# New due times, lags and look-ahead for the planner that orders an attention and expert-routing kernel

## The chip, the cores and the metric

One core of one Trainium2 chip runs the whole program. The metric is the device time of one execution in microseconds, as the median of several runs; a profile of one further execution shows where the time lies.

## The reference, cut to what matters

The input `x` is 8 batches of 512 tokens of 512 numbers in float32. The layer is cross-attention followed by a routed feed-forward part:

```python
def reference(x, ctx, mask, Wq, bq, Wk, bk, Wv, bv, Wo, bo, Ws, bs, W1, b1, W2, b2):
    xn = layernorm(x)                                 # per token
    q, k, v = xn @ Wq + bq, ctx @ Wk + bk, ctx @ Wv + bv
    # 16 heads of 32; sim = q k^T / sqrt(32), masked by key
    x = x + softmax(sim) @ v @ Wo + bo
    xf = layernorm(x).reshape(4096, 512)
    route_prob = softmax(xf @ Ws + bs).T              # 8 experts x 4096 tokens
    route_vals, routes = top_k(route_prob, 512)       # each expert takes 512 tokens
    h = gelu(einsum('ekd,edf->ekf', xf[routes], W1) + b1)      # 2048 wide
    y = (einsum('ekf,efd->ekd', h, W2) + b2) * route_vals
    return x + scatter_add(y at routes)
```

## The kernel before, in words

**Two stages.** The attention stage handles all 8 batches and also writes the normalised rows and the routing logits; the expert stage then picks each expert's tokens, gathers them and runs the two expert products. Every float32 operand of a product is split into a high and a low part (names ending in hi and lo), and a product is three matmuls: high by high, low by high, high by low. The expert stage isn't touched by the change.

**The unit of the attention stage is a group** of four heads of one batch: 32 groups, g = 4b + r for batch b. For a group there are these steps, each of which may have a part on several engines:
- `proj` k and q (lines 1883 to 1885): 12 matmuls each in four chunks; ScalarE makes the high part (line 1266), VectorE the low part (line 1475); SyncE stores both in HBM (`keep_hi`, `keep_lo`, lines 954 and 961) and loads them again in a stacked layout (`stack_hi`, `stack_lo`, lines 985 and 996; `mask_row`, line 971).
- `max`, 16 tiles (line 1901): scores of queries by keys; VectorE takes the extremum of each row (line 1490) and ScalarE the sum of exponentials (`sum`, line 1289).
- `rows` (line 1918): the 16 columns of extrema are turned into rows; ScalarE (line 1280) and VectorE (line 1498, `rows_lo`) split them, and GpSimd issues two small DMAs (line 1183) that put them under the stacked queries. The first `score` of the group waits for these.
- `score`, 16 tiles (line 1933), whose exponentials ScalarE makes (line 1301), and `att`, four steps of four matmuls each (line 1944; eight records a step in the trace), that add into one bank; `recip`, `rden` (line 1925), `divide` (line 1522) and `osplit` (lines 1310 and 1546) finish the group.

**Per batch** come four tiles each of: `load c`, `csplit` (ScalarE line 1246, VectorE line 1426) for the context; `load x`, `stats` (VectorE lines 1394 to 1398, then GpSimd line 1043), `norm` (line 1403), `turn` (PE line 1843) for the queries' input; `v`; and after the batch's groups `residual` (line 1114), `add_bias` (line 1141), `outa` and `out` (PE lines 1960 to 1962, VectorE lines 1554 and 1562 with statistics behind the latter), `x1_norm`, `route` (PE line 1975), `logits` (line 1986) and `back` (line 1994). The loads of c, x and residual share four slots in turn (line 1103 for c and x): a c tile of batch b can only be loaded when the residual tile of batch b - 2 has been routed and its normalised row stored (SyncE line 1018).

**What sets the order.** Each engine executes its steps in the order of a list, in program order, and waits on semaphores. The list comes from a planner in Python that runs when the kernel is built (`Plan`, `attention_agenda`). Every step has a due time counted in groups, a cost on its engine and a time until others see its result (`COST`), and the steps it comes after. Steps of one kind on one engine form a line in order of due time; in the simulated time of the planner, an engine takes, of all heads of lines that can start within `LOOK` microseconds of the earliest, the one that is due first. So due times decide only where several steps are ready together. PSUM banks are given out by the same plan, and at most three `max` and two `score` tiles are held at a time (`HELD`). The due time of a step is its place in `K_AT`, `Q_AT`, `MAX_AT` (one pair for each place of a group in its batch) or `SPAN` (group offset, first and last of the four tiles), plus the engine's `LAG` for that line. The costs are fixed numbers. The steps before group 0's first scores are written out by hand (`first_steps`), and the change doesn't reach them.

```python
first = min(start for start, _ in able)
start, part = min((p for p in able if p[0] <= first + LOOK), key=lambda p: (p[1].at, p[0]))
```

Of the kernel before, what the change touches and what calls it, by code (L numbers as in the profile page):

```python
# [71 lines left out]
class Plan:  # L72
# [14 lines left out]
    def run(self):  # L87
# [36 lines left out]
        while left:  # L124
            best = None
            for engine in a.order:
# [7 lines left out]
                if able:  # L134
                    first = min(start for start, _ in able)
                    start, part = min((p for p in able if p[0] <= first + LOOK), key=lambda p: (p[1].at, p[0]))
                    if best is None or start < best[0]:
# [128 lines left out]
def first_steps(a):  # L266
# [101 lines left out]
             "piece_in": (0.800, 3.00)},  # L368
}
STATISTICS = (1.020, 1.10)  # L370
LOOK = 0.0482
HELD = {"max": 3, "score": 2}
LAG = {
    ("act", "proj"): 0.05484, ("dve", "proj_lo"): 0.02698, ("pool", "rows_lo"): -0.63573, ("act", "rows"): 0.02773, ("dve", "rows_lo"): -0.36946,
    ("sync", "stack_hi"): -0.05651, ("sync", "stack_lo"): 0.367, ("pool", "recip"): -0.23075, ("dve", "rden"): -0.1455, ("dve", "outa"): -0.82589,
    ("dve", "csplit_lo"): 0.10561, ("dve", "turn_lo"): 0.12437, ("dve", "v"): 0.35108, ("dve", "out"): 0.28505, ("act", "turn"): -0.2497,
    ("dve", "back"): 0.11423, ("act", "osplit"): -0.38468, ("dve", "divide"): 0.38329, ("act", "logits"): -0.64673, ("pool", "add_bias"): -0.82451,
    ("act", "csplit"): -0.35997, ("pe", "rows"): 0.22469, ("dve", "route"): -0.24839, ("dve", "max"): -0.0842, ("dve", "recip"): 0.22088,
    ("act", "score"): 0.05782, ("act", "sum"): 0.03391, ("pe", "score"): -0.3388, ("dve", "osplit_lo"): 0.25044, ("sync", "den_in"): 0.01022,
    ("sync", "den_out"): -0.08642,  # L380
}
K_AT = ((0.29686, 0.40376), (-0.04542, 0.29441), (0.02773, 0.08012), (-0.31589, 0.13175))
Q_AT = ((0.44226, 0.47919), (0.23484, 0.31819), (0.08741, 0.37171), (0.25863, 0.4367))
MAX_AT = ((-0.0746, 0.65113), (-0.03252, 0.72888), (-0.08586, 0.78647), (0.28673, 0.73702))
ROWS_AT, RECIP_AT, RDEN_AT, OSPLIT_AT, ATT_AT = -0.39061, 0.33435, 1.07093, -0.39162, 0.06092
SPAN = {
    "v": (-1, 0.20496, 1.61489), "load_c": (-3, -0.37589, 0.1772), "csplit": (-3, -0.77777, -0.28119), "load_x": (-3, 0.70516, 0.81243),
    "stats": (-3, 0.5984, 0.6084), "norm": (-3, 0.59116, 1.14657), "turn": (-3, 0.37171, 0.50368), "residual": (2, -0.16222, 0.44313),
    "add_bias": (2, 1.63304, 2.37175), "outa": (2, 0.17666, 1.03948), "out": (4, 0.05675, 0.7842), "x1_norm": (4, 0.60213, 1.17617),
    "route": (4, 0.40306, 1.08729), "logits": (4, 0.55598, 1.13947), "back": (4, 0.74368, 1.13342),  # L390
}


def spread(span, k, n):
    return span[0] + (span[1] - span[0]) * (k + 0.5) / n


def attention_agenda():
# [48 lines left out]
    for g in range(NG):  # L447
# [3 lines left out]
        if g >= 2:  # L451
            for w in "kq":
                span = (K_AT if w == "k" else Q_AT)[before]
                turned = [("dve", "turn_lo" if w == "q" else "csplit_lo", b, t) for t in range(TB)]
# [15 lines left out]
        if g >= 1:  # L470
            stacks = [("sync", "stack_" + k, w, g) for k in ("hi", "lo") for w in "kq"] + [("sync", "mask_row", g)]
            for n in range(AHEAD if g == 1 else 0, HG * TB):
                h, t = divmod(n, TB)
                at = g - 1 + spread(MAX_AT[(g - 1) % GB], n, HG * TB)
                p.add("pe", ("max", g, h, t), at, stacks if n == 0 else [], takes=("max", g, h, t))
# [1737 lines left out]
```

## Time and profile before

| | |
|---|---|
| Median of 3 runs | 1664.97 us (1664.57 to 1665.52) |
| Time of the profiled execution | 1665.4 us |
| Its span in the profile | 1663.6 us |
| Granted TensorE clock, mean share | 0.985 |
| TensorE busy | 1596.0 us (96%) |
| VectorE busy | 1120.7 us (67%) |
| ScalarE busy | 979.1 us (59%) |
| GpSimd busy | 299.8 us (18%) |
| First score of group 0, divide of group 31 | 51.63 us, 877.25 us |

Times are counted from the span's start. A busy share of TensorE counts overlapping records, so a stretch of 96% isn't one in which nothing can be gained, and small gaps are better read from single rows. The profiled execution took 1.8 us more than its span, and lies 0.4 us above the median.

### The profile page before, as it was taken

The numbers are of one execution on the slowest core, as the hardware profiler recorded it, in microseconds if no ns is written. First come the engines' busy times: TensorE is split into PE (matmuls) and PEld (weight loads), VectorE is DVE, ScalarE is ACT, GpSimd is POOL, SyncE is SP. The second block draws the span as 40 slices with busy tenths as digits, with TensorE's granted clock in tenths as the row PEclk, the third lists the DMA queues.
The fourth block names the chain that finished last, engine by engine and source line by source line (L and its number), as shares of the span: only waits on it lengthen the run. The fifth ranks groups of instructions, "written<-read, shape, count | busy, mean of one in ns | idle before, by whom it ended". The sixth has DMA issues, their size and how long they took to land.

```text
span 1663.6 us, 22350 instructions
## 1 busy us (share of the span) xinstructions
PE 1596.0 (96%) x7826; PEld 1159.4 (70%) x7826; DVE 1120.7 (67%) x1976; ACT 979.1 (59%) x2119; POOL 299.8 (18%) x396
## 2 busy tenths in 40 slices
PE   7899999999999999999986999999999999999997
PEld 5556666666666666666543777888888888888885
DVE  7677877968789697886846588665554555454543
ACT  5788898998989989899873223222232323232331
POOL 6220221302213022130300201002020202020100
PEclk9999999999999999999998999999999999999998
DMA  5643654736446365463521323416252524343330
GB/s 179 171 123 104 192 147 145 197 91 195 139 145 198 90 196 143 140 185 93 182 85 64 128 91 100 147 51 184 76 159 102 158 95 140 102 135 117 100 112 26
DMA packets 131271, 217.27 MB, mean 131 GB/s; under 512 B 17116, under 2 KB 51056, under 8 KB 131160
## 3 DMA queue, kind: packets, MB, share of 16 engines
q1 hardware_dynamic: 114520, 173.23, 33.2%
q0 software_dynamic: 16640, 42.61, 9.8%
q8 instruction: 63, 1.03, 0.3%
q14 instruction: 48, 0.39, 0.1%
HBM read 157.45 MB, written 57.82 MB: 129 GB/s over the span
## 4 chain that ended last, share of the span: by engine, by line
PE 86%; DVE 7%; DMA 2%; ACT 2%; issue 1%; POOL 0%; SPq 0%; ACTq 0%; DVEq 0%; POOLq 0%
PE ps_gen L894 9%; PE ps_gen L895 8%; PE ps_gen L896 8%; PE ps_gen L1933 7%; PE ps_gen L2101 7%; PE ps_gen L2102 7%; PE ps_gen L2103 7%; PE ps_gen L1901 7%; PE ps_att L1944 7%; PE ps_gen L1883 3%; PE ps_gen L1884 3%; PE ps_gen L1885 3%; PE ps_gen L1960 2%; PE ps_gen L1961 2%; PE ps_gen L1962 2%
## 5 line engine op out<-in xcount | busy, mean ns | idle before, releaser
L1490 DVE TENSOR_REDUCE nmax<-ps_gen 128x1 f32<-128x512 f32 x512 | 331.5, 683 | 76.4 <-PE ps_gen L1901 74.9
L1301 ACT ACTIVATE p_ring<-ps_gen,keep_scale 128x512 f32<-128x512 f32 x512 | 342.8, 706 | 45.9 <-PE ps_gen L1933 32.6
L1289 ACT ACTIVATE ps_gen<-ps_gen,nmax 128x512 f32<-128x512 f32 x512 | 344.0, 681 | 32.6 <-DVE nmax L1490 32.4
L1363 ACT ACTIVATE gel<-ps_gen,b_cols 128x512 f32<-128x512 f32 x128 | 88.3, 690 | 446.4 <-PE ps_gen L896 438.3
L1765 DVE TENSOR_TENSOR gel_lo<-gel,gel_hi 128x512 fp32r<-128x512 f32 x126 | 87.2, 692 | 269.0 <-ACT gel_hi L1364 264.6
L1901 PE MATMUL ps_gen<-kst,qst 97*128 97x512 f32 x512 | 192.5, 423 | 9.2 <-issue 5.4
L1933 PE MATMUL ps_gen<-qst,kst 99*128 99x512 f32 x512 | 196.6, 427 | 3.7 <-DMA qst<-by_row 3.2
L894 PE MATMUL ps_gen<-hT_hi,w_hi 128*128 128x512 f32 x504 | 199.2, 395 | 0.0
L2101 PE MATMUL ps_gen<-w_hi,gel_hi 128*128 128x512 f32 x504 | 198.0, 393 | 0.0
L896 PE MATMUL ps_gen<-hT_hi,w_lo 128*128 128x512 f32 x504 | 196.4, 390 | 0.0
L2103 PE MATMUL ps_gen<-w_hi,gel_lo 128*128 128x512 f32 x504 | 196.4, 390 | 0.0
L895 PE MATMUL ps_gen<-hT_lo,w_hi 128*128 128x512 f32 x504 | 196.3, 390 | 0.0
L2102 PE MATMUL ps_gen<-w_lo,gel_hi 128*128 128x512 f32 x504 | 196.2, 389 | 0.0
L1933 PEld LDWEIGHTS ps_gen<-qst,kst 99*128 99x128 f32 x512 | 93.7, 191 | 81.0 <-issue 61.7
L1901 PEld LDWEIGHTS ps_gen<-kst,qst 97*128 97x128 f32 x512 | 95.2, 191 | 78.4 <-issue 48.6
L1211 POOL DMA_INDIRECT out_x<-y_out,idx x28 | 49.5, 1767 | 508.6 <-ACT y_out L1383 502.2
L1944 PE MATMUL ps_att<-p_ring,v_sb 128*32 128x512 f32 x1024 | 138.4, 613 | 0.8 <-ACT p_ring L1301 0.7
L1289 ACT ACTIVATION_READ_ACCUMULATOR ps_gen<-ps_gen,nmax 128x1 f32 x512 | 115.7, 226 | 0.0
L896 PEld LDWEIGHTS ps_gen<-hT_hi,w_lo 128*128 128x128 f32 x504 | 94.6, 188 | 20.4
L2103 PEld LDWEIGHTS ps_gen<-w_hi,gel_lo 128*128 128x128 f32 x504 | 94.6, 188 | 19.9
L2101 PEld LDWEIGHTS ps_gen<-w_hi,gel_hi 128*128 128x128 f32 x504 | 94.8, 188 | 19.2
L894 PEld LDWEIGHTS ps_gen<-hT_hi,w_hi 128*128 128x128 f32 x504 | 94.6, 188 | 19.3 <-issue 0.2
(233 smaller groups left out, 2692.3 us busy)
## 6 DMA issues: line engine op xcount, KB each, us to landing
w_raw<-in_L_ffn_W SPq DMA_DIRECT2D x128, 512.0 KB, 3.2
kst<-qk_rows SPq DMA_DIRECT2D x93, 256.0 KB, 4.1
qst<-qk_rows SPq DMA_DIRECT2D x93, 256.0 KB, 4.2
x_in<-in_x POOLq DMA_DIRECT2D x60, 256.0 KB, 4.0
out_x<-x_in SPq DMA_DIRECT2D x32, 256.0 KB, 3.4
qk_rows<-kT_hi SPq DMA_DIRECT2D x31, 256.0 KB, 2.4
qk_rows<-kT_lo SPq DMA_DIRECT2D x31, 256.0 KB, 3.7
qk_rows<-qT_hi SPq DMA_DIRECT2D x31, 256.0 KB, 2.0
```

Source lines behind the costliest of these rows:

```text
L894: e.matmul(psum, lhsT=wh, rhs=mh, start=(i == 0), stop=False)
L895: e.matmul(psum, lhsT=wh, rhs=ml, start=False, stop=False)
L896: last = e.matmul(psum, lhsT=wl, rhs=mh, start=False, stop=(i == n - 1))
L1289: e.activation(psum[:, :], psum[:, :], ACT.Exp, bias=nmax[g % 2][:, c], scale=-1.0, accum_out=den[g % 2][:, c]).then_inc(drained_sem("max" ...
L1301: e.activation(p_ring[n % NP_][:, :], ps("score", g, kt, h)[:, :], ACT.Exp, scale=keep_scale[:, b:b + 1]).then_inc(drained_sem("score", g, ...
L1490: e.tensor_reduce(nmax[g % 2][:, h * TB + t:h * TB + t + 1], ps("max", g, h, t)[:, :], AX.X, ALU.min).then_inc(s_min, 1)
L1901: e.matmul(ps("max", g, h, t)[:, :], lhsT=qst[k][0:ROWS_MAX, h, t * P:(t + 1) * P], rhs=kst[k][0:ROWS_MAX, h, :], start=True, stop=True).t ...
L1933: e.matmul(ps("score", g, kt, h)[:, :], lhsT=kst[k][0:ROWS_ALL, h, kt * P:(kt + 1) * P], rhs=qst[k][0:ROWS_ALL, h, :], start=True, stop=Tr ...
L1944: last = e.matmul(ps_att[h * DH:(h + 1) * DH, :], lhsT=v_sb[:, kt, (c4 * HG + h) * DH:(c4 * HG + h + 1) * DH], rhs=p_ring[((g * KT + kt) * ...
L2101: e.matmul(ps_y[tt], lhsT=gh, rhs=wh, start=(j == 0), stop=False)
L2102: e.matmul(ps_y[tt], lhsT=gh, rhs=wl, start=False, stop=False)
L2103: return e.matmul(ps_y[tt], lhsT=gl, rhs=wh, start=False, stop=(j == NF - 1))
```

## The change

It replaces constants of the planner and nothing else. `LOOK` goes from 0.0482 to 0.00729. All `LAG` values are new but for one, and three lines that had none get one (`mask_row`, `x1_norm` and `out` on SyncE). All entries of `K_AT`, `Q_AT`, `MAX_AT`, the five single due times, and the spans of all per-batch steps are new. `COST`, `HELD`, the steps, their waits, the tiles and buffers are the same. The new numbers were chosen with transfers and operations of random length; the planner itself still plans with the fixed costs.

```diff
-LOOK = 0.0482
+LOOK = 0.00729
 LAG = {
-    ("act", "proj"): 0.05484, ("dve", "proj_lo"): 0.02698, ("pool", "rows_lo"): -0.63573, ("act", "rows"): 0.02773, ("dve", "rows_lo"): -0.36946,
-    ("sync", "stack_hi"): -0.05651, ("sync", "stack_lo"): 0.367, ("pool", "recip"): -0.23075, ("dve", "rden"): -0.1455, ("dve", "outa"): -0.82589,
-    ("dve", "csplit_lo"): 0.10561, ("dve", "turn_lo"): 0.12437, ("dve", "v"): 0.35108, ("dve", "out"): 0.28505, ("act", "turn"): -0.2497,
-    ("dve", "back"): 0.11423, ("act", "osplit"): -0.38468, ("dve", "divide"): 0.38329, ("act", "logits"): -0.64673, ("pool", "add_bias"): -0.82451,
-    ("act", "csplit"): -0.35997, ("pe", "rows"): 0.22469, ("dve", "route"): -0.24839, ("dve", "max"): -0.0842, ("dve", "recip"): 0.22088,
-    ("act", "score"): 0.05782, ("act", "sum"): 0.03391, ("pe", "score"): -0.3388, ("dve", "osplit_lo"): 0.25044, ("sync", "den_in"): 0.01022,
-    ("sync", "den_out"): -0.08642,
+    ("act", "proj"): 0.01453, ("dve", "proj_lo"): 0.01781, ("pool", "rows_lo"): -0.05858, ("act", "rows"): -0.89192, ("dve", "rows_lo"): -0.8426,
+    ("sync", "stack_hi"): 0.26, ("sync", "stack_lo"): 0.16679, ("pool", "recip"): -0.71984, ("dve", "rden"): -0.21169, ("dve", "outa"): -0.95533,
+    ("dve", "csplit_lo"): 0.26287, ("dve", "turn_lo"): -0.13028, ("dve", "v"): 0.26129, ("dve", "out"): 1.02186, ("act", "turn"): -0.30754,
+    ("dve", "back"): 0.11101, ("act", "osplit"): -0.65589, ("dve", "divide"): 0.38481, ("act", "logits"): -0.23725, ("pool", "add_bias"): -0.98999,
+    ("act", "csplit"): -0.81133, ("pe", "rows"): 0.84674, ("dve", "route"): 0.1247, ("dve", "max"): -0.04206, ("dve", "recip"): 0.2929,
+    ("act", "score"): 0.05782, ("act", "sum"): 0.03446, ("pe", "score"): -0.49348, ("dve", "osplit_lo"): -0.00772, ("sync", "den_in"): -0.07322,
+    ("sync", "den_out"): 0.01316, ("sync", "mask_row"): 0.29139, ("sync", "x1_norm"): -0.20992, ("sync", "out"): 0.12762,
 }
-K_AT = ((0.29686, 0.40376), (-0.04542, 0.29441), (0.02773, 0.08012), (-0.31589, 0.13175))
-Q_AT = ((0.44226, 0.47919), (0.23484, 0.31819), (0.08741, 0.37171), (0.25863, 0.4367))
-MAX_AT = ((-0.0746, 0.65113), (-0.03252, 0.72888), (-0.08586, 0.78647), (0.28673, 0.73702))
-ROWS_AT, RECIP_AT, RDEN_AT, OSPLIT_AT, ATT_AT = -0.39061, 0.33435, 1.07093, -0.39162, 0.06092
+K_AT = ((0.34698, 0.34698), (0.046, 0.34322), (-0.10961, 0.33491), (-0.6045, 0.30063))
+Q_AT = ((0.49169, 0.50358), (0.35419, 0.38821), (0.839, 0.84485), (0.33472, 0.5512))
+MAX_AT = ((0.07646, 0.63787), (-0.02598, 0.72721), (-0.20476, 0.8183), (0.29371, 0.73775))
+ROWS_AT, RECIP_AT, RDEN_AT, OSPLIT_AT, ATT_AT = -1.11808, 0.02837, 1.13556, -0.37311, 0.05184
 SPAN = {
-    "v": (-1, 0.20496, 1.61489), "load_c": (-3, -0.37589, 0.1772), "csplit": (-3, -0.77777, -0.28119), "load_x": (-3, 0.70516, 0.81243),
-    "stats": (-3, 0.5984, 0.6084), "norm": (-3, 0.59116, 1.14657), "turn": (-3, 0.37171, 0.50368), "residual": (2, -0.16222, 0.44313),
-    "add_bias": (2, 1.63304, 2.37175), "outa": (2, 0.17666, 1.03948), "out": (4, 0.05675, 0.7842), "x1_norm": (4, 0.60213, 1.17617),
-    "route": (4, 0.40306, 1.08729), "logits": (4, 0.55598, 1.13947), "back": (4, 0.74368, 1.13342),
+    "v": (-1, 0.20382, 1.58823), "load_c": (-3, 0.30662, 0.67954), "csplit": (-3, -1.70224, -1.44797), "load_x": (-3, 0.83148, 0.99161),
+    "stats": (-3, 0.8562, 0.8662), "norm": (-3, 0.7104, 1.36265), "turn": (-3, 0.41487, 0.53882), "residual": (2, 0.74472, 1.4678),
+    "add_bias": (2, 3.65366, 3.84978), "outa": (2, -0.00032, 1.07505), "out": (4, 0.16207, 0.88416), "x1_norm": (4, 0.67431, 1.26815),
+    "route": (4, 0.19181, 0.92991), "logits": (4, 0.61262, 1.15474), "back": (4, 0.69917, 1.19967),
 }
```

## Rows read from the trace of the kernel before

**Rows 1.** Windows, a batch each: us, busy us of each engine, PEclk

```profile
367.15:471.62 104.47, 102.58 (x537) 67.08 (x537) 84.26 (x161) 94.40 (x222) 22.77 (x36) 1.00 0.52 153
575.00:678.35 103.35, 102.63 (x538) 67.07 (x537) 84.41 (x161) 94.68 (x222) 22.77 (x36) 1.00 0.53 154
678.35:784.95 106.60, 104.20 (x537) 68.27 (x537) 84.00 (x161) 94.59 (x222) 22.71 (x36) 0.98 0.51 150
```

**Rows 2.** Waits of the span: who, for whom, total us, times, longest

```profile
PE ps_gen L1933 <- DMA qst<-by_row: 3.2, 3, 1.7
...
PE ps_gen L1883 <- DVE kT_lo L1475: 3.3, 6, 0.6
```

**Rows 3.** The chain that ended last, 60 to 84 us: start, us, what

```profile
64.32 0.52 ACT wo_hi L1253
64.83 0.59 ACT qT_hi L1266
...
65.44 5.36 DMA qk_rows<-qT_hi
...
71.16 7.48 DMA qst<-qk_rows
```

**Rows 4.** Timeline of PE near 80 us: start, us, engine, line, what [idle before]

```profile
80.08 1.19 PE L1901 MATMUL ps_gen<-kst,qst 97*128 97x512 f32 x2 [5.07 <-issue]
```

**Rows 5.** Granted clock by stretch, columns as in rows 1

```profile
77.00:84.00 7.00, 3.92 (x13) 2.56 (x17) 4.47 (x7) 5.95 (x13) 1.07 (x2) 0.51 0.91 253
```

**Rows 6.** Timeline of VectorE, 309 to 313 us

```profile
309.85 0.68 DVE L1394 BATCH_NORM_STATS2 stat<-x_in 128x6 f32<-128x512 f32 x1
...
310.86 0.69 DVE L1394 BATCH_NORM_STATS2 stat<-x_in 128x6 f32<-128x512 f32 x1
...
311.87 0.68 DVE L1490 TENSOR_REDUCE nmax<-ps_gen 128x1 f32<-128x512 f32 x1
```

**Rows 7.** Timeline of PE, 309.9 to 312 us

```profile
309.97 0.39 PE L1901 MATMUL ps_gen<-kst,qst 97*128 97x512 f32 x1
```

**Rows 8.** Timeline of GpSimd, 414 to 423 us

```profile
417.61 1.18 POOL L1183 DMA_DIRECT2D qst<-by_row  x2 [1.77 <-DVE by_row L1498]
418.77 2.17 POOL L1114 DMA_DIRECT2D x_in<-in_x  x4
```

**Rows 9.** Timeline of PE, 417 to 423 us

```profile
421.94 0.47 PE L1933 MATMUL ps_gen<-qst,kst 99*128 99x512 f32 x1 [1.18 <-DMA qst<-by_row]
```

**Rows 10.** Timeline of GpSimd, 694 to 708 us

```profile
701.48 0.56 POOL L1043 TENSOR_TENSOR rstd<-rstd,half 128x1 f32<-128x1 f32 x1 [2.67 <-DVE rstd L1398]
705.15 1.04 POOL L1183 DMA_DIRECT2D qst<-by_row  x2 [3.11 <-issue]
```

**Rows 11.** Timeline of PE and VectorE, 700 to 712 us

```profile
703.24 0.54 DVE L1403 TENSOR_SCALAR x_in<-x_in,mv,rstd 128x512 f32<-128x512 f32 x1
...
707.48 0.70 PE L1933 MATMUL ps_gen<-qst,kst 99*128 99x512 f32 x2 [1.69 <-DMA qst<-by_row]
```

**Rows 12.** Timeline of GpSimd, 284 to 290 us

```profile
287.39 1.04 POOL L1183 DMA_DIRECT2D qst<-by_row  x2 [0.24 <-issue]
```

**Rows 13.** Timeline of all engines, 296 to 304 us

```profile
296.28 0.55 POOL L1103 DMA_DIRECT2D x_in<-in_ctx  x1 [3.97 <-DMA hn_rows<-x_in]
...
301.09 0.68 DVE L1426 TENSOR_TENSOR cT_lo<-x_in,cT_hi 128x512 fp32r<-128x512 f32 x1
...
302.31 0.74 DVE L1475 SCALAR_TENSOR_TENSOR kT_lo<-ps_gen,bias_cols,kT_hi 128x512 fp32r<-128x512 f32 x1
...
303.11 0.50 PE L1883 MATMUL ps_gen<-cT_hi,wk_hi 128*128 128x512 f32 x1 [0.54 <-DVE kT_lo L1475]
```

**Rows 14.** Timeline of SyncE, 812 to 836 us

```profile
824.75 0.38 SPq L954 DMA_DIRECT2D qk_rows<-qT_hi  x1
...
828.83 0.79 SPq L985 DMA_DIRECT2D qst<-qk_rows  x2
```

**Rows 15.** Timeline of PE, 816 to 843 us

```profile
834.21 0.97 PE L1901 MATMUL ps_gen<-kst,qst 97*128 97x512 f32 x3 [1.76 <-DMA qst<-qk_rows]
```

## The prediction

> **What bounds the kernel now.** I read four views in this order: busy time in windows of one batch, the waits, the chain that ended last, and timelines of the places that the chain names. The windows show that the attention stage repeats itself: an ordinary batch of four groups (the one from 575.00) takes 103.35 us [rows 1], so a group takes 103.35 / 4 = 25.84 us. TensorE is busy in 102.63 of them and ScalarE in 94.68, so TensorE sets the pace, ScalarE is close behind, and a new order of the same work can only win back idle time. Two batches are longer: 104.47 us, which is 1.1 over, and 106.60 us, which is 3.2 over [rows 1]. The waits name what they have in common: scores that wait for `by_row`, 3 times and 3.2 us in all [rows 2]. The same view gives the regular wait at the border of two batches, TensorE for VectorE's `kT_lo`, 6 times and at most 0.6 us [rows 2]. Beside these there are two irregular places, the start (groups 0 to 2) and the last groups, where steps run out. The expert stage isn't touched, and I take its time as fixed.
>
> **How the due times act.** A due time decides only where several steps are ready together on one engine. TensorE runs projections as filler long before they are due, so I don't follow each constant; I go to the places where the trace shows idle time or a close race, and ask there which of two ready steps now comes first. `LOOK` falls from 48 to 7 ns: I cost it at nothing. Its cover is that an engine with a backlog has several steps ready at the same moment; were that gone, it would cost or save at most 0.04 us a choice. The lags of SyncE likewise: its queue is mostly idle, its steps go when their data is there, and the late ones are late by their transfers. Deadlines of GpSimd (`recip`, `add_bias`, loads) order an engine that is busy 22.77 of 103.35 us [rows 1]; nothing, as long as the slots come free at the same times.
>
> **Part 1, the start.** The chain goes over ScalarE's `wo_hi` (0.52 us), then `qT_hi` of group 2, its store of 5.36 us and the load of 7.48 us [rows 3], and TensorE stands for 5.07 us before the first `max` of group 2 [rows 4]. Its clock is at 0.51 of full speed from 77 to 84 us, that is at the lower of its two levels for nearly the whole stretch, after the idle time began [rows 5]. The second `wo` tile is due at 0.4 + 0.12 = 0.52 in both versions. `qT_hi` was due at 0.4746 + 0.0548 = 0.529, behind it; it is now due at 0.5021 + 0.0145 = 0.517, ahead of it. That takes one `wo_hi` out of the chain: -0.5 us. The transfers are as slow as before, so the idle time shrinks and doesn't go. Bounds: -2.5 (half of the idle time, if the stores find quieter queues) and +2 (one more transfer of four caught in front, nearest row 7.48 - 5.36 = 2.1 us).
>
> **Part 2, statistics of x against the last extrema** (groups 2, 6, 10 and so on). VectorE runs two statistics steps of about 1.0 us each, at 309.85 and 310.86, and only at 311.87 the last extremum of group 10 [rows 6], whose matmul started at 309.97 [rows 7]. At 310.86 both were ready. Before, the statistics were due at 9.600 to 9.608 and that extremum at 9.705 - 0.084 = 9.621; now it is 9.857 or later against 9.704 - 0.042 = 9.662. The extremum goes first, and everything behind it, `rows` and the `by_row` transfers, is 1.0 us earlier. In group 14 the pair of transfers is issued at 417.61 and directly behind it come four loads of the residual tiles [rows 8]; the score starts only at 421.94 after 1.18 us of idle TensorE [rows 9]. 1.0 us of this is covered: -1.0. In the other five such groups nobody waited, so nothing comes back there. What is late next is the statistics, thus `norm` and `turn`, by one extremum of 0.68 us; fillers cover that (projections of k run there). Bounds: -1.2 and 0.
>
> **Part 3, the stall in group 25.** GpSimd ends `rstd` at 702.04 and issues `by_row` only at 705.15, 3.11 us for which no releaser is found [rows 10]; TensorE waits 1.69 us [rows 11], and the batch is 3.2 us longer. The same pair of steps in group 9 shows 0.24 us [rows 12], so the stall isn't part of the order. If it comes from where an instruction stands in a queue, it may remain; if it is chance, it will rarely fall on a step with so little slack. I take the likelier, that it doesn't hurt again: -3.2, with 0 as the other end. The Trainium skill (SBUF — State Buffer, "SBUF: two separate sides") says that a VectorE operation in a two-port mode keeps GpSimd from writing descriptors for its whole length. By that rule the stall could be no longer than the SBUF to SBUF step beside it, which took 0.54 us [rows 11]; the trace, with 3.11 us, doesn't agree that this lock is the cause, and with such a stall alone removed the sum would have -0.5 in place of -3.2.
>
> **Part 4, the border of batches.** The fourth context tile is loaded at 296.28 after 3.97 us of waiting for the stored normalised row, its low part runs at 301.09, `kT_lo` at 302.31, and the next batch's projection starts at 303.11 [rows 13]. `kT_lo` keeps its distance to the extrema that it races: due 0.306 + 0.018 = 0.324 against 0.327 - 0.042 = 0.285 for the eighth, before 0.279 against 0.324 - 0.084 = 0.240. So 0 here. The other steps of the steady part I also cost at 0, between -0.7 a batch (0.54 idle and as much again as a gated start adds) and +1.3 a batch (rival A).
>
> **Part 5, the last groups.** The q projection of group 31 was due at 29.24 to 29.31, now at 29.36 to 29.38: 0.08 to 0.11 groups, 2.0 to 2.9 us. It heads the chain at the end: stored at 824.75, loaded at 828.83 [rows 14], and TensorE waits 1.76 us for it [rows 15]. TensorE has gaps there and will take the filler early, so I count +1.0, between -2 (ScalarE's `proj` lag is 0.04 groups, 1.0 us, shorter, for k and for q) and +2.9.
>
> **Sum.** -0.5 - 1.0 - 3.2 + 0 + 1.0 = -3.7 us. From the profiled execution's 1665.4 this gives 1661.7; that execution lies 0.4 above the median, so 1661.3.
>
> **Rivals.**
> A, slower: the routing chain. `out`'s last tile on TensorE is due at 4.794 in place of 4.693, 0.10 groups or 2.6 us later, and VectorE's part of it has a lag of 1.02 in place of 0.29, which gives way to every extremum. Behind it hang the stored row, the slot, the context tile and the projection [rows 13]. That tile's low part ends at 301.77 and its user starts at 303.11, so there are 1.3 us to spare. It decides from the point where the delay is over that and TensorE has no filler: 2.6 - 1.3 = 1.3 us a batch, in 6 batches 7.8: 1669.1. Against it speaks that the q projection of the same time is later too and fills.
> B, no change: the stall of GpSimd stays or a like one hits another step. Without the -3.2: 1664.5. For it speaks that the three runs lie within 1 us, as if it were in each.
> C, faster by more: the borders lose their waits (6 x 0.7 = 4.2) and the start another 2.5: 1654.6. For it speaks that numbers chosen against random lengths leave more room before exactly such waits; against it that ScalarE has only 8.7 us free in a batch.
> D, VectorE holds GpSimd up: `by_row` is issued at another moment, and if GpSimd can't issue while VectorE runs the normalising step of 0.54 us [rows 11], each of 7 groups with little slack may pay it, +3.8: 1665.1. Rows 12 speak against it, with an issue after 0.24 us. It is what the page of the Trainium skill named in part 3 would have, in the same section.
> E: the lists come out the same where it matters, 1665.0.
>
> **How the numbers follow.** A measurement can tell about 0.2% from no change, 3.3 us. The forecast has 0.36, C 0.20, B 0.21, A 0.17, D 0.04, E 0.02. The forecast's own range is 1658 to 1664, and 0.26 of its 0.36 lies below 1661.6; with C that is 0.46 faster. Its other 0.10, B, and most of D and E make 0.35 the same. A and 0.02 from the tails of the bounds make 0.19 slower. The range goes from just under C, 1653, to just over A, 1670; beyond lie part 2 to 5 at their bad ends together.
>
> **What would show it.** Right: batches of 103.3 us throughout, no score waiting for `by_row`, and statistics of x behind the last extremum in groups 2, 6, 10. `qT_hi` of group 2 before the second `wo_hi`, and the idle time near 80 us under 5 us but not gone. Wrong: a batch's length moved by more than 0.5 us in all batches alike (then the steady order matters, A or C), projections at the border waiting for a context tile, a GpSimd gap of about 3 us at the same count of instructions, or more idle time before the first `max` of group 31.

## The result and the profile after

| | before | changed |
|---|---|---|
| median of the runs, us | 1664.05 (20 runs, 1659.24 to 1666.86) | 1667.56 (20 runs, 1665.02 to 1675.47) |
| ratio to before, 95% interval | | 1.0027 (1.0018 to 1.0037) |
| profiled execution, us | 1665.4 | 1665.48 |
| span, us | 1663.6 | 1663.7 |
| mean granted clock | 0.985 | 0.990 |

The change makes the kernel 3.5 us slower in the median, 0.27%. I had forecast 1661.3, faster. The profiled execution of the changed kernel is one of its quickest, 2.1 us under its median; a second profile of the same kernel (experiment e4 below) has a span of 1671.1 us. I use both.

A gain and a loss of 8 us cancel in this profile. First its windows, one batch each, from the first score of group 4 on (columns as in [rows 1]):

```profile
155.71:261.41 105.70, 103.17 (x537) 66.91 (x536) 84.43 (x162) 94.10 (x221) 22.73 (x36) 1.00 0.51 151
261.41:365.91 104.50, 102.88 (x537) 66.92 (x536) 83.67 (x162) 93.95 (x221) 22.84 (x36) 1.00 0.53 153
365.91:471.14 105.23, 102.98 (x538) 67.03 (x536) 83.69 (x162) 94.03 (x221) 23.09 (x36) 1.00 0.51 151
471.14:576.21 105.07, 102.97 (x537) 67.02 (x536) 83.58 (x162) 94.04 (x221) 23.10 (x36) 1.00 0.51 152
576.21:681.61 105.40, 102.96 (x537) 66.99 (x536) 83.60 (x162) 93.98 (x221) 22.71 (x36) 1.00 0.51 151
681.61:788.42 106.81, 103.27 (x538) 66.94 (x536) 84.99 (x162) 94.11 (x221) 22.74 (x36) 1.00 0.49 149
```

Group 4 starts at 155.71 us; before it started at 163.68. The start gained 7.97 us. The six batches last 632.71 us, and they lasted 624.73 (163.68 to 788.41): 7.98 us lost, between 0.2 and 2.4 us in each, where before only two were long [rows 1]. The engines do the same work in each batch. TensorE is busy for 617.12 us of the six before and for 618.23 now, so its idle time grows from 7.6 to 14.5 us: nearly 7 of the 8 us. What follows group 28 differs by 0.1 us.

The waits of TensorE in the steady part, 155 to 830 us (who, for whom: total us, times, longest), of the changed kernel:

```profile
PE ps_gen L1933 <- DMA qst<-by_row: 8.1, 7, 1.4
PE ps_gen L1901 <- ACT ps_gen L1289: 3.9, 7, 0.6
```

Scores waited for `by_row` 2 times and 2.9 us in this stretch before (3 times and 3.2 us in the whole span [rows 2]); now it is 7 times and 8.1 us: group 25 as ever, and one new wait in each batch, in groups 7, 11, 15, 19, 23 and 27. That is 5.2 of the 8 us. `kT_lo` is gone as a releaser at the border of batches [rows 2, 13]; the extremum's buffer (`L1901 <- ACT`) is the regular wait in its place, and the two are worth about the same. The other 2.8 us of the batches are not traced to a cause here.

Here is one new wait, group 11, in the timeline of SyncE, GpSimd and TensorE of the changed kernel:

```profile
332.85 0.40 PE L1933 MATMUL ps_gen<-qst,kst 99*128 99x512 f32 x1
...
333.29 0.78 SPq L985 DMA_DIRECT2D kst<-qk_rows  x2
334.11 0.43 SPq L996 DMA_DIRECT2D kst<-qk_rows  x1
334.41 0.99 POOL L1183 DMA_DIRECT2D qst<-by_row  x2 [0.88 <-DVE by_row L1498]
334.58 0.57 SPq L971 DMA_DIRECT2D kst<-mask_rows  x1
339.20 0.70 PE L1933 MATMUL ps_gen<-qst,kst 99*128 99x512 f32 x2 [0.84 <-DMA qst<-by_row]
```

and the same place in the kernel before:

```profile
338.89 0.40 PE L1933 MATMUL ps_gen<-qst,kst 99*128 99x512 f32 x1
339.32 0.57 SPq L971 DMA_DIRECT2D kst<-mask_rows  x1
339.34 1.00 POOL L1183 DMA_DIRECT2D qst<-by_row  x2
339.94 0.92 SPq L985 DMA_DIRECT2D kst<-qk_rows  x2
340.89 0.43 SPq L996 DMA_DIRECT2D kst<-qk_rows  x1
```

SyncE's three k stacks of group 13 (256 KB each) used to be issued 0.6 us behind group 11's two `by_row` transfers of 8 KB; now they go out 1.1 us ahead of them. What frees SyncE is the same in both, group 10's last score (the first line of each); 0.4 us later it issues. Before, `mask_row` took the first 0.6 us of that, and `by_row` came 0.45 us after the score. Now the stacks come first, and `by_row` 1.56 us after it. The time from issue to landing of just these two transfers, changed and then before (the row of the view of line 1183, 333 to 341 and 338 to 343 us):

```profile
DMA to landing us min/median/max: 4.1/4.1/4.2
```

```profile
DMA to landing us min/median/max: 1.7/1.9/2.1
```

So the steps of VectorE and TensorE are 5 us earlier than before, and 2.2 us of that are lost on the transfer. The chain of the changed kernel between 333 and 345 us goes over it (start, us, what):

```profile
334.91 4.16 DMA qst<-by_row
```

The view of the DMA queues shows part of the delay: from 334.40 to 336.55 us it has 302 packets of SyncE's queue and not one of GpSimd's, at a DMA share of 100.7%. The first packet of `by_row` starts 2.2 us after its issue; before it started after 1.1 us.

At the start, the chain of the changed kernel, and TensorE before group 2's first `max`:

```profile
62.25 0.52 ACT wo_hi L1253
...
65.35 0.58 ACT qT_hi L1266
...
65.97 5.15 DMA qk_rows<-qT_hi
...
71.49 5.02 DMA qst<-qk_rows
```

```profile
77.34 0.93 PE L1901 MATMUL ps_gen<-kst,qst 97*128 97x512 f32 x3 [2.03 <-DMA qst<-qk_rows]
```

The store takes as long as before (5.15 us against 5.36), the load 5.02 us against 7.48 [rows 3], and the idle time falls from 5.07 [rows 4] to 2.03 us. The clock then stays up. The window that had 0.51 [rows 5], and a later one, both of the changed kernel:

```profile
77.00:84.00 7.00, 6.00 (x30) 3.87 (x31) 6.15 (x10) 5.42 (x13) 0.89 (x2) 1.00 1.02 289
94.00:101.00 7.00, 7.00 (x41) 4.78 (x40) 6.41 (x13) 7.00 (x19) 2.94 (x4) 1.00 0.56 166
```

Before, a second stretch at the lower level followed; here the granted clock is 1.00 up to group 4. The later window in the kernel before:

```profile
94.00:101.00 7.00, 6.83 (x23) 3.83 (x23) 5.50 (x12) 5.42 (x15) 1.14 (x2) 0.52 0.00 0
```

Seven microseconds at 0.51 and seven at 0.52 owe 7 x (0.49 + 0.48) = 6.8 us of work. Up to group 4 TensorE is busy 143.56 us in the kernel before and 137.21 us in the changed one, with 627 and 626 matmuls: 6.4 of the 8 us of the start are the clock, and 1.6 us are less idle time. That the second stretch too came from the 5.07 us of idle time is not shown; TensorE was busy 6.50 of the 7 us before it.

And GpSimd in group 25:

```profile
701.52 0.55 POOL L1043 TENSOR_TENSOR rstd<-rstd,half 128x1 f32<-128x1 f32 x1 [2.09 <-DVE rstd L1398]
705.20 1.03 POOL L1183 DMA_DIRECT2D qst<-by_row  x2 [3.13 <-issue]
```

The stall that I had taken for chance is there again [rows 10], 3.13 us for 3.11. So is its cost: the score of group 25 waits 1.40 us, where it waited 1.69.

### The profile page after: what moved, and what is told of

It reads as the page before. It is cut to its first block, busy times and chain, and to the rows that moved or that the text cites. A ratio compares the mean times of both kernels' runs of the same rounds, so it can differ in the third digit from the quotient of the medians.

```text
span 1663.7 us, 22371 instructions
## 1 busy us (share of the span) xinstructions
PE 1592.6 (96%) x7826; PEld 1154.2 (69%) x7826; DVE 1120.2 (67%) x1976; ACT 975.7 (59%) x2119; POOL 298.6 (18%) x396
## 4 chain that ended last, share of the span: by engine, by line
PE 75%; DVE 8%; ACT 8%; DMA 5%; issue 2%; POOL 1%; SPq 0%; ACTq 0%; POOLq 0%; DVEq 0%
PE ps_gen L894 8%; PE ps_gen L895 8%; PE ps_gen L896 8%; PE ps_gen L2101 7%; PE ps_gen L2102 7%; PE ps_gen L2103 7%; PE ps_gen L1933 6%; PE ps_att L1944 5%; PE ps_gen L1901 5%; ACT ps_gen L1289 4%; ACT p_ring L1301 2%; DVE nmax L1490 2%; DMA qst<-by_row 2%; PE ps_gen L1883 2%; PE ps_gen L1884 2%
## 5 line engine op out<-in xcount | busy, mean ns | idle before, releaser
L1289 ACT ACTIVATE ps_gen<-ps_gen,nmax 128x512 f32<-128x512 f32 x512 | 348.7, 691 | 35.0 <-DVE nmax L1490 34.7
L1901 PE MATMUL ps_gen<-kst,qst 97*128 97x512 f32 x512 | 193.0, 422 | 7.3 <-ACT ps_gen L1289 4.7
L1901 PEld LDWEIGHTS ps_gen<-kst,qst 97*128 97x128 f32 x512 | 95.0, 190 | 68.1 <-issue 24.1
L1289 ACT ACTIVATION_READ_ACCUMULATOR ps_gen<-ps_gen,nmax 128x1 f32 x512 | 121.5, 237 | 0.0
```

The costliest lines, as they stand in the source:

```text
L1289: e.activation(psum[:, :], psum[:, :], ACT.Exp, bias=nmax[g % 2][:, c], scale=-1.0, accum_out=den[g % 2][:, c]).then_inc(drained_sem("max" ...
L1901: e.matmul(ps("max", g, h, t)[:, :], lhsT=qst[k][0:ROWS_MAX, h, t * P:(t + 1) * P], rhs=kst[k][0:ROWS_MAX, h, :], start=True, stop=True).t ...
```

## The experiments

Two theories of the lost 8 us. **Queue**: `by_row` of groups 3 mod 4 is late because SyncE's k stacks are ahead of it. **Lateness**: VectorE's last extrema (`MAX_AT`, `max` lag) come later in their group, and the transfer is incidental. For the 3.1 us stall: chance, or tied to something countable. Each ratio is to runs of the kernel before that were made beside it.

**e1, the k stacks wait for `by_row`**, in the changed kernel. SyncE holds the k stack of groups 1 mod 4 until the row maxima of the group two before have landed:

```diff
                     w, g = at
+                    if w == "k" and g % GB == 1 and g > GB:
+                        on.wait_ge(s_maxrow[(g - 2) % NST], 32 * ((g - 2) // NST + 1))
                     on.wait_ge(s_kept_hi[w], 16 * g)
```

> The changed kernel, with one wait more: SyncE issues the stacked k loads of groups 5, 9, 13 and so on only when the by_row rows of the group two before (7, 11, 15 and so on) have landed. Theory Q (queueing): in groups 3 mod 4 the two small by_row transfers are issued 0.5 to 1.1 us behind three stacked loads of 256 KB and take 3.7 to 4.1 us instead of about 1; with the wait they land within 1.7 us of the second issue, TensorE no longer waits for them there (0.8 to 1.4 us each, 6 times), batches fall from 105.1 to about 103.9 us, and the time is 6 us below the changed kernel, near 1661.5. Theory L (lateness): the extrema of these groups are due later (0.818 for 0.786) and the rows are simply late; the waits stay above 0.8 us, batches at 105 us, the time at 1667.5 or above, because the loads come later too.

Measured: 1662.10 us, ratio 0.9986 (0.9974 to 0.9998), 9.5 us below the changed kernel in the same job (e4). Batches 105.35, 103.83, 104.22, 105.18, 103.63, 105.1 us. Group 11 again, timeline and landing:

```profile
334.19 1.00 POOL L1185 DMA_DIRECT2D qst<-by_row  x2 [0.88 <-DVE by_row L1500]
336.41 0.78 SPq L987 DMA_DIRECT2D kst<-qk_rows  x2
```

```profile
DMA to landing us min/median/max: 1.7/1.7/1.7
```

```profile
PE ps_gen L1935 <- DMA qst<-by_row: 1.7, 2, 1.5
```

The maxima are hardly earlier (0.2 us), the transfer takes 1.7 us in place of 4.1, and 8.1 us of waits become 1.7. The queue theory holds, lateness falls. The six batches come to 627.3 us in this profile, 5.4 us less than in the changed kernel's first; 2.6 us over the kernel before stay.

**e2, one pair of due times back**: the changed kernel with `MAX_AT[2]` of before.

```diff
+MAX_AT = MAX_AT[:2] + ((-0.08586, 0.78647),) + MAX_AT[3:]
```

> The changed kernel with one pair of due times set back, MAX_AT[2] from (-0.20476, 0.8183) to (-0.08586, 0.78647), the rest as changed. It turns the order of the race round: by_row of groups 3 mod 4 is then issued before the stacked k loads instead of behind them. Theory Q: batches of 103.3 to 103.7 us, no wait for by_row in groups 3 mod 4, 1660 to 1662 us. Theory L: the same here, since the extrema are earlier too; the first run tells the two apart. If the loss of the steady part is spread over many due times instead, batches stay at 104.5 or more and the time at 1666 or more.

Measured: 1680.64 us, ratio 1.0097 (1.0081 to 1.0114).

```profile
339.94 1.00 POOL L1186 DMA_DIRECT2D qst<-by_row  x2 [12.19 <-DVE by_row L1501]
339.98 0.78 SPq L988 DMA_DIRECT2D kst<-qk_rows  x2
```

```profile
DMA to landing us min/median/max: 3.3/3.6/4.0
```

```profile
PE ps_gen L1936 <- DMA qst<-by_row: 12.5, 7, 2.0
```

A miss, and one that sharpens the picture: issued at the same moment as the stacks `by_row` still takes 3.6 us. Before, `mask_row` took 0.6 us on SyncE ahead of the stacks, and `by_row` was issued in them. That this is what let it through is argued and not shown: no run set the pair and `mask_row` back together.

**e3, the kernel before with the new due time of `stats` alone.**

```diff
+SPAN['stats'] = (-3, 0.8562, 0.8662)
```

> The kernel before with SPAN['stats'] alone changed to (-3, 0.8562, 0.8662), part 2 of the prediction by itself. If that part's reasoning holds (one local race, everything behind it 1 us earlier), by_row of groups 2 mod 4 lands 1 us earlier and the time is that of before or up to 1 us less. If a due time acts through the whole order that the planner builds, the steady batch changes by several us either way; a batch over 105 us and a time over 1680 would show that single constants can't be costed one by one.

Measured: 1702.07 us (one run), first full batch 112.95 us. A constant of such a set, changed alone, costs ten times what the whole set does; that it was good or bad in the set can't be read from it. Its profile shows the same crossing, without the changed `MAX_AT` or lags: from group 11 on the first k stack is issued 0.6 us ahead of `by_row`, which takes 4.0 to 5.3 us; in group 7 it comes 3 us behind, and nobody waits.

```profile
PE ps_gen L1936 <- DMA qst<-by_row: 13.7, 6, 2.7
```

That is 10.8 us more than before, about a quarter of what the six batches lose here (665.5 us for 624.7); the rest isn't traced.

**e4, the changed kernel again**, for a second profile.

> The changed kernel unaltered, for a second profile. The batches and the waits for by_row (6 groups, 0.8 to 1.4 us each) come back as they were if they belong to the order; the start (idle 2.03 us near 77 us, clock at full speed to 830 us) may differ if it hangs on how long single transfers take: then a run with a longer idle time there shows the clock at its lower level behind it and a time 5 us or more above 1665.5.

Measured: 1671.56 us, ratio 1.0024 (1.0010 to 1.0038); batches 105.79, 105.17, 106.14, 105.45, 105.13, 109.19 us, group 4 at 156.87 us.

```profile
PE ps_gen L1933 <- DMA qst<-by_row: 9.8, 7, 3.1
```

The loss in the batches is larger here, 12.1 us, and another 2.2 us are lost behind the first score of group 28, against 6.8 gained at the start: 7.5 us, which is the difference of the spans (1671.1 for 1663.6). It fits the median above before. The order of issue is the same as in the first profile (stacks 1.1 us ahead), and `by_row` takes 3.6 to 4.8 us in the six groups, for 4.1 to 4.6 there.

**e6, e2's pair with e1's waits.**

> The changed kernel with MAX_AT[2] of before and SP's waits on the row maxima. Queue theory: e2's 15.0 us of waits for by_row came from k stacks of group g + 2 that overtake it; with the waits they fall below 4 us, batches go from 105.3 to 107.2 down to about 103.5 to 104.5, and the total to 1659 to 1665, 16 to 20 us below e2. If MAX_AT[2] itself was what cost e2 its 11 us (lateness of the maxima), the total stays above 1672.

Measured: 1663.18 us, ratio 0.9986 (0.9973 to 0.9999), 17 us below e2 (0.9986 for 1.0097, each by its own runs of before); batches 103.59, 103.52, 104.17, 104.08, 104.13, 105.15 us.

```profile
PE ps_gen L1938 <- DMA qst<-by_row: 1.4, 1, 1.4
```

The one wait left is group 25's. As the queue theory said; the pair itself costs nothing in the time, and the six batches, 624.6 us, are as long as in the kernel before.

**e8, the kernel before with e1's waits.**

> The kernel before with SP's waits on the row maxima, which in the changed kernel took 9.5 us. Queue theory: in the kernel before by_row is not overtaken (SP issues the k stacks 0.6 us or more behind it), so the waits bring nothing: within 1.5 us of before, waits for by_row 2 to 4 us as before. If the waits help for another reason (SP's queue in general), before gains several us too.

Measured: 1664.33 us, ratio 0.9989 (0.9979 to 1.0000), 1.2 us below before in its job, and `by_row` waits of 1.7 us. Where nothing overtakes, the waits bring 1.2 us with an interval that touches none.

**e10, `mask_row`'s lag undone** in the changed kernel, which puts it ahead of the stacks again and changes no other due time.

```diff
+LAG["sync", "mask_row"] = 0.0
```

> The changed kernel with one lag undone (mask_row's, 0 instead of 0.291), which in the planner's order moves mask_row of every group ahead of its k stacks again and changes no due time else. mask_row takes 0.57 us of SP's issue, the k stacks of g + 2 then come 0.5 us ahead of by_row of groups 3 mod 4 instead of 1.1 us. Queue theory: 512 KB ahead still hold by_row up, since any lead is enough; waits for by_row 6 to 11 us, batches 104.5 to 105.5, total within 3 us of the changed kernel's. If the place of mask_row is what matters, by_row lands within 1.5 us and batches come to 103.5 to 104, total 1660 to 1663.

Measured: 1673.01 us, ratio 1.0049 (1.0032 to 1.0065).

```profile
333.83 0.58 SPq L974 DMA_DIRECT2D kst<-mask_rows  x1
...
334.45 0.92 SPq L988 DMA_DIRECT2D kst<-qk_rows  x2
334.95 1.00 POOL L1186 DMA_DIRECT2D qst<-by_row  x2 [0.88 <-DVE by_row L1501]
```

```profile
DMA to landing us min/median/max: 4.2/4.6/5.0
```

With the lead cut from 1.1 to 0.5 us the transfer is as slow (4.6 us), as the queue theory said. The waits for `by_row` are 12.2 us, over the 6 to 11 that I gave them, and batches of 105.3 to 111.9 us are longer than I gave; the total is 1.4 us above e4's, but the ratio is 0.0025 above (1.0049 for 1.0024, by 4 runs). Sorted by lead of the stacks, `by_row` of group 11 takes: 1.1 us ahead 4.1; 0.5 ahead 4.6; at the same moment 3.6; 0.6 behind 1.9; 2.2 us behind, when it has landed, 1.7. The first three overlap over the groups of their profiles (4.1 to 4.6, 4.1 to 5.0, 3.3 to 4.4), so how far the stacks are ahead can't be read from them, only that they aren't behind.

**e7, the start of the kernel before, with later loads held.**

```diff
                     slot_free(key)
+                    if (what, b, t) == ("c", 1, 3):
+                        on.wait_ge(s_stack_hi["q"][2], 32)
```

> The kernel before, with GpSimd's load of ctx tile 3 of batch 1 (and the loads behind it) held until the first two q stacks of group 2 have landed. Contention theory of the start: the stack transfers of 7.48 us share the engines with 256 KB loads; without two of them they land in about 5 us, the idle time before group 2's first maxima goes from 5.07 to about 2.5 us, TensorE's clock stays at its upper level, score 0 of group 4 starts 5 to 8 us earlier and the total is 3 to 8 us lower, unless the later loads make batch 1's split late. Rival (order theory): the start gained by what the planner put around the projections of group 2, not by the transfers; the idle time stays within 1 us of 5.07 and the total within 1.5 us.

Measured: 1663.12 us, ratio 0.9990 (0.9976 to 1.0004). The held loads went out at 79.79 us and later. Its chain and TensorE's timeline:

```profile
72.13 7.05 DMA qst<-qk_rows
```

```profile
79.98 1.19 PE L1903 MATMUL ps_gen<-kst,qst 97*128 97x512 f32 x2 [3.96 <-DMA qst<-qk_rows]
```

The load stays at 7.05 us though behind it nothing large was issued but the third q stack, 1.2 us later, and e8, with further loads behind it, has 6.88. Transfers behind it don't explain the length. Those issued ahead are left. The idle time fell by 1.1 us, the first score of group 4 came at 164.79 us, and the time is 0.1% lower with an interval over none; neither of my two theories had quite this, and holding the later loads doesn't give the gain of the start. GpSimd before, then changed:

```profile
67.95 0.54 POOL L1103 DMA_DIRECT2D x_in<-in_ctx  x1 [4.88 <-DVE wo_lo L1463]
70.38 0.54 POOL L1103 DMA_DIRECT2D x_in<-in_ctx  x1 [1.89 <-DVE wo_lo L1463]
```

```profile
64.18 0.54 POOL L1103 DMA_DIRECT2D x_in<-in_ctx  x1 [2.51 <-DVE wo_lo L1463]
70.31 0.54 POOL L1103 DMA_DIRECT2D x_in<-in_ctx  x1 [5.59 <-DVE by_row L1498]
```

The q stack of group 2 is issued at 70.8 and 71.1 us. Before, two context loads were in flight then, and the third k stack too (issued at 66.97, landed 6.8 us later). In the changed kernel the earlier context load had gone out 3.8 us sooner and the k stack 1.35 us sooner, and both had landed: one load of 256 KB is left of three. That fits the 2.5 us; it was not tried alone. All four profiles with the three in flight (before, e3, e7, e8) have 6.44 to 7.48 us for this load, and all ten with one have 4.07 to 5.02.

**The stall of GpSimd.** In the profiles of before, after, e1 to e4, e6 to e8 and e10 it precedes `by_row` of group 25, at 701 to 736 us, and is 3.11 to 3.17 us long. Its place among GpSimd's recorded instructions differs by 5 between before and after (367 and 372 ahead of it), its time by 34 us between e1 and e3. What is the same in all ten is that it is the 129th transfer that GpSimd issues (the pair of `by_row` counts as two). Three kernels issue four transfers more.

e5, e1's kernel with four transfers of one row of 32 bytes each, before batch 0 (at 16 us):

```diff
+                    for n in range(4):
+                        e.dma_start(spare[n:n + 1, :], x_tok[0:1, 0:8]).then_inc(s_spare, 16)
```

> The kernel with SP's waits on the row maxima (e1) and four more transfers of 128 bytes that GpSimd issues before batch 0's first score. Count theory: GpSimd stands still for 3.1 us at its 129th transfer whatever that is; here that is one of the two by_row transfers of group 24 (its scores start about 2.9 us after the rows land, so it costs 0.3 us or nothing), and group 25's by_row is issued in 1 us. Batch 6 (scores of group 24 to group 28) goes from 105.1 us to 103.6 to 104.3, the total 0.8 to 1.5 us below e1's. Chance theory (of my prediction) or a theory of the place in the program (the stall belongs to group 25's by_row): the stall stays at group 25, batch 6 and the total as e1's.

Measured: 1663.01 us, ratio 0.9987 (0.9973 to 1.0001). GpSimd:

```profile
701.69 1.03 POOL L1189 DMA_DIRECT2D qst<-by_row  x2 [3.13 <-issue]
```

A miss: it stays, now at the 133rd, and the 129th, group 24's `by_row`, is issued 0.75 us after VectorE's step. e9, e6's kernel with four transfers of 128 rows, in groups 5 to 8 (183 to 259 us):

```diff
+                    if 5 <= g < 9:
+                        if g > 5:
+                            on.wait_ge(s_spare, 16 * (g - 5))
+                        e.dma_start(spare[:, :], Wo[0:P, 0:64]).then_inc(s_spare, 16)
```

> e6's kernel (MAX_AT[2] of before, waits on the row maxima) with four more transfers on GpSimd, one each in groups 5 to 8, of 128 rows of 256 bytes (32 KB). e5 showed that four transfers of a single 32-byte row don't move the 3.1 us stall from group 25's by_row, so it isn't the number of transfers. If it comes after a number of rows (descriptors) that GpSimd has written, a 256 KB tile of 128 rows counting as one of these, the stall moves four tile loads back, to a load of x near 620 us, where nothing waits for it; batch 6 goes from 105.15 to about 103.5 and the total to 1 to 2 us below e6. If it comes after a number of bytes, it moves one load back, to the context load at 691 us. If it belongs to the place in the program, it stays at by_row of group 25 at 700 us.

Measured: 1655.43 us, ratio 0.9946 (0.9930 to 0.9963), by 4 runs. GpSimd in groups 24 and 25:

```profile
673.95 0.96 POOL L1194 DMA_DIRECT2D qst<-by_row  x2 [24.65 <-issue]
...
698.47 1.03 POOL L1194 DMA_DIRECT2D qst<-by_row  x2 [0.27 <-issue]
```

Group 25's is issued without a stall, which none of my three theories had. The 129th is now group 24's: it is issued 1.8 us after VectorE's step ahead of it ended, where e6 has 0.5, and group 24 has time (in e6 3 us between landing and score). e11, the same places, one row each:

```diff
-                        e.dma_start(spare[:, :], Wo[0:P, 0:64]).then_inc(s_spare, 16)
+                        e.dma_start(spare[0:1, :], Wo[0:1, 0:64]).then_inc(s_spare, 16)
```

> e9's kernel with its four extra transfers cut from 128 rows to one row of 256 bytes, in the same places (groups 5 to 8). e5 (one row each, at 16 us) left the 3.1 us stall at group 25's by_row, e9 (128 rows each, 183 to 259 us) took it away from there and left 1.3 us at group 24's by_row. If the rows decide, the 3.1 us stall is at group 25's by_row here, the 133rd transfer, and the total is that of e6, 1.5 to 4 us above e9's kernel in this job. If the place in time decides (or the order among the other transfers), group 25's by_row is issued within 0.3 us and the total is e9's.

Measured: 1658.68 us, ratio 0.9962 (0.9951 to 0.9974).

```profile
695.90 1.03 POOL L1194 DMA_DIRECT2D qst<-by_row  x2 [0.27 <-issue]
```

As in e9, with 1.8 us at the 129th, as I had expected if the place decides: neither rows nor bytes do. e12 is e9 once more:

> e9's kernel once more, beside e11 on one chip, in more rounds. If its gain is its own and not the chip's or the run's, the ratio to before is 0.993 to 0.9965 again and group 25's by_row is again issued without a stall; if e9's 0.9946 was drawn from few runs, the ratio goes to e6's 0.9986.

Measured: 1659.10 us, ratio 0.9964 (0.9951 to 0.9977), group 25 without a stall again. The first ratio was a little flattered by its few runs; the gain over before is real. Over e6 it is less sure: 0.9964 and 0.9962 for 0.9986, with intervals that just overlap (down to 0.9973 there, up to 0.9977 and 0.9974 here). With four more transfers between 183 and 259 us the stall of 3.1 us is gone and 1.3 us more stand at a step with slack; with four at 16 us it stays. Why those at 16 us don't count stays open.

e11 and e12 are the best versions: 0.36% under before, some 6 us, and about 0.6% under the changed kernel.

## Why the prediction was wrong

**Part 4, the steady order, is the step that failed.** I looked at one race at the border, `kT_lo`, and there I was right: about nothing. But I costed "the other steps of the steady part" at 0 and, in the first part, the lags of SyncE at nothing, because "its queue is mostly idle". The queue in which SyncE issues may be mostly idle; the transfers in it are not independent of GpSimd's. `mask_row` got a lag of +0.29, which put it behind the k stacks, and the extrema of groups 3 mod 4 end 1.1 us later against the score that frees SyncE; so the k stacks of g + 2 crossed `by_row` of g. Either alone is enough to spoil it (e10 has the first undone, e2 the second). The price is 2.2 us on a transfer that had 0.5 to 0.9 us of slack, once a batch. This term was 0 with bounds of -0.7 to +1.3 a batch (no run shows what the -0.7 adds for a "gated start"). The waits for `by_row` grew by 5.2 us over six batches in the first profile and by 6.9 in e4's. In all, parts 2 and 3 among it, the six batches lost 8.0 us, 1.3 a batch, in one profile, and 12.1, 2.0 a batch, in the other, where I had -4.2 for parts 2 to 4 together; about 3 us of the 8 stay without a traced cause. "A batch's length moved by more than 0.5 us in all batches alike" was the sign that I had named.

**Part 3 failed too.** The stall isn't chance: -3.2 forecast, 0 measured. Rival B had this. Its evidence was luck: the three runs lay within 1 us, but twenty of the same kernel lie between 1659.24 and 1666.86. What speaks for it is the stall in ten of ten profiles. It wasn't at the same count of instructions, the sign that I had named, but at the same count of transfers. The test by the Trainium skill's rule on the shared port stands: the stall is as long as before, 3.13 us, where the step beside it had 0.54 [rows 11] and no single VectorE step in it is over 0.7 us, so the trace still speaks against that lock.

**Part 1 had the sign and not the size or the reason.** -0.5 forecast, -8.0 measured in this profile (-6.8 in e4), beyond my bound of -2.5. `qT_hi` didn't overtake the second `wo_hi`: at 65.35 us it is half a microsecond later than before. The gain begins with the shorter load, which I had as the outer bound ("if the stores find quieter queues"), and most of it is the clock, which I read in rows 5 and left out of the sum: 6.4 us less of busy time for the same matmuls. In the ten profiles with the changed kernel's start the idle time ahead of this `max` is 1.5 to 2.8 us and group 4 starts at 155.5 to 158.9; in e7 and e8, with the start of before, the idle time is 3.96 and 5.29 us and group 4 starts at 164.8 and 163.0.

**Part 2 had the order right; that its wait is gone is luck.** The last extremum now runs ahead of the statistics; VectorE in group 10 of the changed kernel [rows 6]:

```profile
304.60 0.68 DVE L1490 TENSOR_REDUCE nmax<-ps_gen 128x1 f32<-128x512 f32 x1
305.20 0.68 DVE L1394 BATCH_NORM_STATS2 stat<-x_in 128x6 f32<-128x512 f32 x1
```

and group 14's wait of 1.18 us [rows 9] is gone. But e7 and e8, which keep the order of before, have no such wait either: there the second `by_row` of group 14 landed after 2.1 and 2.0 us, and after 3.5 in the one profile that I had read. So the -1.0 took a slow transfer of one execution for a cost of the order, and the new order isn't shown to be worth anything here.

**Part 5** came to +0.1 for a forecast +1.0: the stand before group 31's first `max` [rows 15] is gone, and one of 1.76 us stands ahead of an `att` step at 832.98 us in its place.

**Rival A** had "slower" for another reason: the routing chain. No projection of the six batches waits for a context tile in the changed kernel. Its total of 1669.1 is near the measured one by accident.

Sum by measured terms, first profile: start -8.0, batches +8.0, end +0.1: span 1663.7 for 1663.6. My forecast for these three was -0.5, -4.2 and +1.0, so two errors of 7.5 and 12.2 us in part cancel: in this profile the sum is off by 3.8 us, and the medians say +3.5 for my -3.7. That the batches lose more than the start gains in the median execution is what e4's profile shows (-6.8, +12.1, +2.2).

## What to carry to other kernels

Look at transfers of all issuing engines in one list, ordered by issue, before costing a change in order: here a small transfer that a matmul waits for took 2 us longer when large ones of another engine went out just ahead of it. A planner that gives a transfer a fixed length, or a random one drawn for each by itself, can't see this, and can trade half a microsecond of order for two of waiting; a wait on the small transfer's semaphore ahead of the large ones cost nothing here. And a stall that sits in one profile at one instruction should be looked for in a second profile before it is called chance.

## What the hardware did that I had not expected

- Two transfers of 8 KB, issued by GpSimd, land 4.1 us after issue with 768 KB issued by SyncE up to 1.1 us ahead, 4.6 us with the stacks up to 0.5 us ahead, 3.6 us when issued together, 1.9 us when they are themselves 0.6 us ahead, 1.7 us with the stacks held back. The Trainium skill (DMA: Bandwidth & Descriptors, "Queues, rings and completion order") says that each DMA engine goes round its queues packet by packet. By that rule a small transfer in a queue of its own would wait for about one packet of the other each time its turn comes. The rows show 1.9 to 2.9 us more than with the stacks held back, and 2.2 us until the first packet of GpSimd's queue where 1.1 is usual; no run shows how long a packet in the page's sense is, so they neither bear the rule out nor refute it.
- The load of a 256 KB stack took 7.05 us with one large transfer issued behind it and three in flight ahead, 6.88 (e8) and 7.48 us with more behind it and the same three ahead, and 5.02 us with one in flight ahead.
- GpSimd stood for 3.1 us at its 129th transfer in ten of ten profiles. With four further transfers at 16 us it stood as long at the 133rd; with four after 183 us 1.3 us more stood at the 129th and nothing at the 133rd, in three profiles.
- The start's 5.07 us of idle TensorE were followed by two stretches at the lower level, seven microseconds at 0.51 and seven at 0.52; 2.03 us by none in the first profile. In the second (e4) 1.55 us of idle time were followed by a granted clock of 0.84 from 77 to 88 us, 1.8 us owed, and in e5 2.78 us by none: the length of this idle time alone doesn't tell what the clock does behind it.
